# A two-layer adaLN network on one core: last stage reordered around batch 0, small weights turned earlier, rank in three operations

## The reference, cut to what matters

```python
x = x + ga * L0_attn(h);  x = x + gb * L0_ffn(h)        # layer 0, batch 2, 512 rows, 512 wide
x = x + ga1 * L1_attn(h)                                # layer 1, 128 heads of 4+64, out @ Wo
h = layernorm(x) * (1 + cb1) + sb1
# L1_ffn(h):
base_out = h @ base_W.T + base_b                        # 512 x 512
probs = softmax(h @ router_W.T + router_b)              # 15 entries
topk_p, topk_i = top_k(probs, 8)                        # ties: lower index first
w[expert_map[topk_i]] += topk_p                         # 8 experts
hr = h @ A.T                                            # 8 experts x rank 16 = 128 columns
x = x + gb1 * (base_out + (hr * w) @ B * 2)
```

## Time and profile before

| | |
|---|---|
| median of 3 runs | 2178.25 us |
| profiled execution, its own time | 2175.61 us |
| its span | 2173.8 us |
| granted TensorE clock, mean over the span | 0.994 of full speed |
| TensorE busy | 2122.4 us (98%) |
| VectorE / ScalarE / GpSimd busy | 1732.3 / 1341.9 / 1357.7 us |
| chain that ended last, share of TensorE / VectorE | 87% / 7% |

### The profile page before, as it was taken

One profiled execution on the slowest core, in us unless ns is written; L12 is line 12 of the kernel. 1 busy time (PEld: TensorE's weight loads), 2 busy tenths in 40 slices (PEclk: granted clock), 3 DMA queues, 4 the chain that ended last, 5 costly groups with the idle time before them and its releaser, 6 DMA issues.

```text
span 2173.8 us, 42824 instructions
## 1 busy us (share of the span) xinstructions
PE 2122.4 (98%) x11276; PEld 1644.1 (76%) x11276; DVE 1732.3 (80%) x3095; ACT 1341.9 (62%) x2709; POOL 1357.7 (62%) x1621
## 2 busy tenths in 40 slices
PE   7999999999999999999999999999999999999978
PEld 4788888888886757777777777777777777777756
DVE  6787788788777758888888888888888877788764
ACT  2443443433433568888888888888888865555532
POOL 4766766766753447777777777777777721365334
PEclk9999999999999999999999999999999999999999
DMA  7010010010004153222222222222222222444441
GB/s 249 26 43 30 20 48 29 19 48 29 19 20 121 37 189 108 71 73 78 74 78 65 77 78 74 76 66 79 75 77 69 75 79 76 138 130 124 114 130 40
DMA packets 138991, 165.82 MB, mean 76 GB/s; under 512 B 30261, under 2 KB 72917, under 8 KB 138916
## 3 DMA queue, kind: packets, MB, share of 16 engines
q1 hardware_dynamic: 135076, 152.31, 24.5%
q0 software_dynamic: 3840, 12.59, 2.0%
HBM read 101.52 MB, written 29.10 MB: 60 GB/s over the span
## 4 chain that ended last, share of the span: by engine, by line
PE 87%; DVE 7%; issue 2%; ACT 1%; POOL 1%; SPq 1%; DMA 1%; DVEq 0%; ACTq 0%; POOLq 0%
PE bank L2593 12%; PE bank L2578 11%; PE bank L2600 11%; PE bank L2155 7%; PE bank L2157 7%; PE bank L2156 7%; PE bank L2510 6%; PE bank L2508 5%; PE bank L2509 5%; PE bank L2623 3%; PE bank L2633 3%; PE bank L2628 2%; DVE rope_b L1631 1%; DVE rope_a L1630 1%; DVE rope_b L1632 1%
## 5 line engine op out<-in xcount | busy, mean ns | idle before, releaser
L1934 DVE TENSOR_REDUCE mcol<-bank 128x1 fp32r<-128x512 f32 x1024 | 684.1, 687 | 186.8 <-PE bank L2578 176.7
L2593 PE MATMUL bank<-q,k 128*128 128x512 f32 x1024 | 417.9, 408 | 0.0
L2578 PE MATMUL bank<-km,q 128*128 128x512 f32 x1024 | 406.0, 397 | 3.5 <-ACT q L1374 2.5
L2600 PE MATMUL bank<-q,k 128*128 128x512 f32 x1024 | 404.0, 395 | 0.0
L2578 PEld LDWEIGHTS bank<-km,q 128*128 128x128 f32 x1024 | 317.6, 310 | 53.0 <-DVE mcol L1934 3.9
L1413 ACT ACTIVATE pT<-bank 128x512 f32<-128x512 f32 x416 | 228.1, 602 | 113.7 <-PE bank L2600 111.9
L1413 ACT ACTIVATE x<-bank 128x512 f32<-128x512 f32 x416 | 227.7, 601 | 88.7 <-PE bank L2600 86.5
L2593 PEld LDWEIGHTS bank<-q,k 128*128 128x128 f32 x1024 | 192.3, 188 | 84.7 <-issue 27.9
L2600 PEld LDWEIGHTS bank<-q,k 128*128 128x128 f32 x1024 | 192.9, 188 | 31.7
L2510 PE MATMUL bank<-hT_hi,wr_lo 128*128 128x512 f32 x512 | 205.5, 401 | 0.0
L2508 PE MATMUL bank<-hT_hi,wr_hi 128*128 128x512 f32 x512 | 202.3, 395 | 0.1
(11 more groups left out here) (372 smaller groups left out, 5061.5 us busy)
## 6 DMA issues: line engine op xcount, KB each, us to landing
q<-q SPq DMA_DIRECT2D x256, 128.0 KB, 2.3
wst<-in_L_attn_Wq_rope SPq DMA_DIRECT2D x64, 256.0 KB, 3.1
o_d<-ost SPq DMA_DIRECT2D x63, 256.0 KB, 3.1
st_q<-in_L_attn_wq SPq DMA_DIRECT2D x8, 1024.0 KB, 7.6
st_wo<-in_L_attn_wo SPq DMA_DIRECT2D x8, 1024.0 KB, 5.4
q<-qc_d SPq DMA_DIRECT2D x256, 32.0 KB
km<-kc_d SPq DMA_DIRECT2D x256, 32.0 KB
k<-kc_d SPq DMA_DIRECT2D x256, 32.0 KB
```

Of the source, the lines that this page charges most:

```text
L1934: dve.tensor_reduce(mcol[:, k % 2, i % 4, i // 4:i // 4 + 1], bank[4 + i % 2][:], AX.X, ALU.max, negate=True)\
L2578: pe.matmul(bank[4 + i % 2][:], q2[:, k % 4, h, i % 4:S:4], km[:, b, h], start=True, stop=True).then_inc(max_mm, 1)
L2593: pe.matmul(bank[s % 4][:], k1[:, k % 2, t], q1[:, k % 4, h], start=True, stop=False)
L2600: pe.matmul(bank[s % 4][:], k2[:, k % 2, h, t], q2[:, k % 4, h], start=False, stop=True).then_inc(scores1, 1)
```

## The change

Four things change, all in the last 100 us.

1. Order. The last sums of batch 0 are loaded first, then x of batch 0, then the sums of batch 1, then x of batch 1. All four `first_heads` and `last_heads` of batch 0 stand ahead of those of batch 1, and the norm and the router of batch 0 ahead of the `last_heads`, respectively the norm, of batch 1. VectorE divides the last sums of batch 1 only behind the rows of norm(3, 0).
2. Small weights. `la` and `rw` have new places in SBUF, are loaded right behind `bw` and share its semaphore; they are turned ahead of the last base weights. The first three `turn_base` stand ahead of the last unit's `sum_unit`. `lb` alone is turned later, behind router(0), and its low part stands behind norm_rows(3, 1).
3. Low rank. ScalarE copies the result of `low_rank_in` to SBUF (`low_rank_copy`) in place of the spread weights (`kept_spread`); VectorE then multiplies in one operation with the factor 2. The normed columns of batch 0 lie in `hT_lo` (high and low parts), those of batch 1 in `hT_hi`.
4. Rank. One subtraction, one comparison with a margin (0 for a lower index, the smallest normal number otherwise) and the count replace two comparisons, a product, a sum and the count.

```diff
+TURN_IN, TURN_OUT, TURN_ROUTER = 4, 5, 6
+TURN_BANKS = (4, 5, 6, 7, 0, 5, 2)
+TURNS1 = (0, 1, 2, TURN_IN, TURN_ROUTER, 3, TURN_OUT)
+HIGH1 = (TURN_IN, 0, 1, 2, 3, TURN_OUT)
+LOW1 = (TURN_IN, TURN_ROUTER, 0, 1, 2, 3, TURN_OUT)
 
...
 
+            def reload_x(b):
+
+                for t in range(TB * b, TB * b + TB):
+                    sp.dma_start(x[:, t], x_d[:, t]).then_inc(x_moved[1 - b], 16)
+
             for u in range(LOOP, UNITS + 1):
                 if u == UNITS - 1:
                     load_last_sums(0)
+                if u == UNITS:
+                    sp.wait_ge(pv1, UNITS - 1)
+                    reload_x(0)
                     load_last_sums(1)
                 period(u, u % 4)
                 if u == UNITS - 5:
@@ -688,15 +717,14 @@
                     sp.wait_ge(qr_mm, UNITS)
                     sp.wait_ge(wr_split, PAIRS)
                     sp.dma_start(bw[:], a["L1_ffn_base_W"].rearrange("(k p) d -> p k d", p=P)).then_inc(wr_loaded[0], 16)
-
-            sp.wait_ge(pv1, UNITS - 1)
-            for t in range(NT):
-                sp.dma_start(x[:, t], x_d[:, t]).then_inc(x_moved[1 - t // TB], 16)
+                    sp.wait_ge(max_mm, 8 * UNITS)
+                    sp.dma_start(la[:], a["L1_ffn_A"].rearrange("e r d -> (e r) d")).then_inc(wr_loaded[0], 16)
+                    sp.dma_start(rw[0:NR], a["L1_ffn_router_W"]).then_inc(wr_loaded[0], 16)
+
+            reload_x(1)
 
 
             sp.wait_ge(o_copied, COPIES)
-            sp.dma_start(la[:], a["L1_ffn_A"].rearrange("e r d -> (e r) d")).then_inc(g_loaded, 16)
-            sp.dma_start(rw[0:NR], a["L1_ffn_router_W"]).then_inc(g_loaded, 16)
             for k in range(KT):
                 sp.dma_start(lb[:, k], a["L1_ffn_B"].rearrange("e (k p) r -> k p e r", p=P)[k]).then_inc(g_loaded, 16)
...
                 act.activation(lh_hi[:, b * S:(b + 1) * S], lh[:, b * S:(b + 1) * S], ACT.Copy).then_inc(r_hhi, 1)
 
+            weights_high1(TURN_IN)
             weights_high1(0)
             weights_high1(1)
             weights_high1(2)
             weights_high1(3)
             sums_high(EARLY)
-            sums_high(EARLY + 1)
             norm_std(3, 0)
-            weights_high1(KT)
-            weights_high1(KT + 1)
             norm(3, 0, (0,))
             norm(3, 0, (1,))
+            norm(3, 0, (2,))
+            sums_high(EARLY + 1)
+            norm(3, 0, (3,))
+            weights_high1(TURN_OUT)
+            router_parts(0)
+            low_rank_copy(0)
             norm_std(3, 1)
-            norm(3, 0, (2,))
-            norm(3, 0, (3,))
             norm(3, 1, (4,))
             norm(3, 1, (5,))
             norm(3, 1, (6,))
             norm(3, 1, (7,))
-            router_parts(0)
             router_parts(1)
+            low_rank_copy(1)
             router_exp()
             kept_turned(0)
             kept_turned(1)
-            kept_spread(0)
-            kept_spread(1)
             low_rank_high(0)
             low_rank_high(1)
...
-                dve.tensor_tensor(cmpg[:], p_m, p_n, ALU.is_gt)
-                chain(dve.tensor_tensor(cmpe[:], p_m, p_n, ALU.is_equal))
-                chain(dve.tensor_tensor(cmpe[:], cmpe[:], before[:].unsqueeze(1).broadcast_to([P, NT, NR, NR]), ALU.mult))
-                chain(dve.tensor_tensor(cmpg[:].rearrange("p t n m -> p (t n m)"), cmpg[:].rearrange("p t n m -> p (t n m)"),
-                                        cmpe[:].rearrange("p t n m -> p (t n m)"), ALU.add))
+                chain(dve.tensor_tensor(cmpe[:], p_m, p_n, ALU.subtract))
+                chain(dve.tensor_tensor(cmpg[:], cmpe[:], margin[:].unsqueeze(1).broadcast_to([P, NT, NR, NR]), ALU.is_ge))
...
             def low_rank_scaled(b):
 
-                dve.wait_ge(r_wexp, b + 1)
-                dve.wait_ge(r_hmm, b + 1)
-                dve.tensor_tensor(lh[:, b * S:(b + 1) * S], bank[1 + b][:], wexp[:, b * S:(b + 1) * S], ALU.mult).then_inc(r_hfull, 1)
+                at = slice(b * S, (b + 1) * S)
+                dve.wait_ge(r_copied, 2 * b + 2)
+                dve.wait_ge(r_wmm, b + 1)
+                dve.scalar_tensor_tensor(lh[:, at], bank[(4, 7)[b]][:], SCALING, lri[:, at], ALU.mult, ALU.mult).then_inc(r_hfull, 1)
 
             def low_rank_low(b):
 
...
             dve.memset(rwT[:], 0.0).then_inc(g_const, 1)
+            weights_low1(TURN_IN)
+            router_weights()
             weights_low1(0)
-            weights_low1(1)
-            weights_low1(2)
-            weights_low1(3)
             last_den(0)
...
+            weights_low1(2)
             gate_attention1(0)
             gate_attention1(1)
-            last_normed(1)
             add_attention1(1)
             gate_attention1(2)
-            last_sums_low(1)
+            norm_stats(3, 0, (0,))
             gate_attention1(3)
-            norm_stats(3, 0, (0,))
             add_attention1(3)
-            gate_attention1(4)
+            weights_low1(3)
             norm_stats(3, 0, (1,))
             norm_stats(3, 0, (2,))
             norm_stats(3, 0, (3,))
+            norm_rows(3, 0)
+            last_den(1)
+            last_normed(1)
+            norm_split(3, 0, (0,))
+            last_sums_low(1)
+            gate_attention1(4)
+            norm_split(3, 0, (2,))
             gate_attention1(5)
-            norm_rows(3, 0)
-            norm_stats(3, 1, (0,))
             add_attention1(5)
             gate_attention1(6)
+            norm_stats(3, 1, (0,))
+            gate_attention1(7)
+            add_attention1(7)
             norm_stats(3, 1, (1,))
-            weights_low1(KT)
-            gate_attention1(7)
-            weights_low1(KT + 1)
             norm_stats(3, 1, (2,))
-            add_attention1(7)
-            norm_split(3, 0, (0,))
             norm_stats(3, 1, (3,))
...
             behind_sums(*turn_at(LOOP))
+            def turn_base(i):
+
+                if i == 0:
+                    pe.wait_ge(wr_loaded[0], 16 * (PAIRS // 2) + 48)
+                    pe.wait_ge(q1_split, UNITS)
+                if i == KT - 1:
+                    pe.wait_ge(o_copied, COPIES)
+                for o in range(KT):
+                    e = pe.transpose(g_bank(i)[:, o * P:(o + 1) * P], bw[:, o, i * P:(i + 1) * P], ident[:])
+                e.then_inc(g_tr, 1)
+
+            def turn_low_rank(i):
+
+                if i == TURN_OUT:
+                    pe.wait_ge(g_loaded, 16 * 9)
+                    pe.wait_ge(wo1_gated, TURN_BANKS[TURN_OUT] + 1)
+                for k in range(KT):
+                    if i == TURN_IN:
+                        e = pe.transpose(g_bank(i)[:, k * P:(k + 1) * P], la[:, k * P:(k + 1) * P], ident[:])
+                    elif i == TURN_OUT:
+                        e = pe.transpose(g_bank(i)[:, k * P:(k + 1) * P], lb[:, k].rearrange("p e r -> p (e r)"), ident[:])
+                    else:
+                        e = pe.transpose(g_bank(i)[:, k], rw[0:NR, k * P:(k + 1) * P], ident[0:NR, 0:NR])
+                e.then_inc(g_tr, 1)
+
             for u in range(LOOP + 1, UNITS + 1):
+                if u == UNITS:
+                    turn_base(0)
+                    turn_base(1)
+                    turn_base(2)
                 before_sums(*turn_at(u))
                 behind_sums(*turn_at(u))
 
 
             def first_heads(t):
                 at = slice(t * P, (t + 1) * P)
-                if t >= KT:
-                    pe.wait_ge(g_lo, t - KT + 1)
+                if t in TURN_BANKS:
+                    pe.wait_ge(g_lo, LOW1.index(TURN_BANKS.index(t)) + 1)
                 for k in range(KT - 1):
                     pe.matmul(bank[t][:], oo_hi[:, k, at], wo1_hi[:, k], start=(k == 0), stop=False)
                     pe.matmul(bank[t][:], oo_hi[:, k, at], wo1_lo[:, k], start=False, stop=False)
...
+            turn_low_rank(TURN_IN)
+            turn_low_rank(TURN_ROUTER)
             turn_base(3)
             pe.wait_ge(wo1_split, KT)
             pe.wait_ge(oo_split, 6)
             first_heads(1)
-            first_heads(5)
+            first_heads(3)
+            first_heads(0)
             first_heads(2)
-            first_heads(0)
-            first_heads(4)
-            last_heads(0)
-            last_heads(1)
-            last_heads(2)
-            first_heads(3)
-            first_heads(6)
-            last_heads(3)
-            last_heads(4)
-            first_heads(7)
-            last_heads(5)
-            last_heads(6)
-            last_heads(7)
-            turn_low_rank(KT)
-            turn_low_rank(KT + 1)
-            norm(3, 0, (0,))
-            norm(3, 0, (1,))
-            norm(3, 0, (2,))
-            norm(3, 0, (3,))
-            turn_low_rank(KT + 2)
-            norm(3, 1, (4,))
-            norm(3, 1, (5,))
-            norm(3, 1, (6,))
-            norm(3, 1, (7,))
+            for t in range(TB):
+                last_heads(t)
+            for t in range(TB, NT):
+                first_heads(t)
+            norm(3, 0)
```

(15 more changed lines are left out.)

152 lines of the change are left out of this document (68 added, 84 removed).

## The result

The changed kernel takes 2185.37 us (median of 7 runs, 2183.42 to 2190.96), the kernel before in the same comparison 2177.45 us (median of 7, 2171.51 to 2180.17). The ratio is 1.0047, 95% interval [1.0031, 1.0062]: 10.2 us slower, 6.8 to 13.5. The ratio goes by the means of the seven runs, 2186.48 and 2176.34 us; the medians lie 7.9 us apart. The forecast was 2183.3 us, 5.05 slower. The direction was right, and the four idle times stand where they were forecast.

A forecast was written before the change was run, and what follows sets the result against it. Only the last stage counts, its end set by `router(1)`'s start, the matmuls behind it and new gaps. +10.4 - 8.5 + 1.8 + 0.9 + 0.3 = +4.9, said 5.0: median 2183.3 us, range 2176 to 2188.

The forecast's parts named there:

- the likeliest case: The forecast itself, with both holes followed by a slow clock: +4.4 to +6.5 us, chance 0.35.
- A: Up to the first matmul with Wo: turns wait 3.5 us for `bw`, slow clock costs 1.7; 2086.6, 4.3 us late.
- B: End of batch 0's part on TensorE: 84 matmuls take 19.7 us to 2106.3, transposes end at 2108.3.
- C: TensorE's new hole ahead of `last_heads(4)`: 5.5 us idle until VectorE's low part at 2113.8, 1.2 GHz expected behind it.
- D: Scaling batch 1's rows: ScalarE's root waits behind the copy of `low_rank_in(0)`; ready at 2128.4, before at 2121.8.
- E: Start of `router(1)`: transposes, three `base` and a slow beginning of 1.7 us put it at 2141.8, +10.4 us.
- F: Behind `router(1)`: 36 matmuls fewer, -8.5 us; exponential waits for copy and table load, new gap of 1.8 ahead of `turn_kept`.
- Tail: Last three `low_rank_out` come close together: +0.9 us for VectorE's gates waiting on GpSimd, +0.3 for two stores.
- Rival 1: TensorE's clock stays at 2.4 GHz: 7.0 us less, so -2.0, 2176.3 us; chance of no fall 0.11.
- Rival 2: Batch 0 first pays: at the turns, `bw` lands under 2078 and the clock holds; 2173.5 us, chance 0.12.
- Rival 3: Longer wait at the turns, `la` and `rw` landing at 2081.5, and longer low clock: +7 to +8, about 2186; chance 0.17.
- Rival 4: On SP's shared list batch 1's sums land about 2095, and GpSimd adds them before x's first tile: under 1 us.

The follow-up runs named there:

- a9: Changed kernel with the small loads issued in the order `rw`, `la`, `bw` in place of `bw`, `la`, `rw`: 2187.30 us, ratio 1.004 to the kernel before.
- a7: Changed kernel with TensorE kept busy in two holes (ahead of the first turn and of `last_heads(4)`) by work that changes nothing: 2183.46 us, ratio 1.0029.
- a8: a6 with batch 1's division at its old early place on VectorE and its `last_heads` ahead of `norm(3, 0)` on TensorE: 2181.03 us, ratio 1.0022.
- a6: Changed kernel with the edits of a1, a3 and a5 together: 2174.22 us, ratio 0.9987 to the kernel before.
- a5: Changed kernel with batch 1's square root ahead of the copy of `low_rank_in(0)`, and `lb`'s low part ahead of `norm_rows(3, 1)`: 2180.43 us, ratio 1.0014.
- a3: Changed kernel with the router's exponential ahead of the copy of `low_rank_in(1)` on ScalarE: 2181.99 us, ratio 1.003.
- c1: a6 with loads ordered `rw`, `bw`, `la`, a semaphore for `la` alone, and `sums_high` of batch 1 one norm column earlier: 2176.25 us, ratio 0.9991.
- a1: Changed kernel with the first three base-weight turns behind the last `sum_unit` again: 2183.28 us, ratio 1.0035.
- a2: Changed kernel with a semaphore of its own for `rw`, waited for only at the turn of `rw`: 2184.43 us, ratio 1.0044.
- c2: a6 with the rank in five operations again: 2180.05 us, ratio 1.0011 to the kernel before.
- b1: Kernel before with only the rank shortened to three operations: 2177.07 us against 2176.21, ratio 1.0006.

## Why the prediction was half right

The measured median lies in the range of 2176 to 2188 us, but outside the likeliest case's own 2182.6 to 2185, and 10.2 us is outside its +4.4 to +6.5. The sum of the forecast was +5.0 for the profiled execution. Counted from the last scores, the last stage is 9.3 us longer. The 4.3 us between are in three terms: 2.0 up to `router(1)`, 1.8 from there to the last matmul, 0.5 in the tail.

- **A, the wait at the turns: right place, wrong load, and this is the first step that failed.** Forecast was an idle time of 3.5 us, ended by `bw`; it was 5.58, ended by `rw`. Two terms were wrong and partly cancelled, which is luck. `bw` was taken at 9.1 us and took 6.3: it landed 0.7 us behind the last scores, so this term was 2.8 too high. `la` and `rw` were taken at nothing, and the wait went on for them for 4.9 us more. I had bounded their cost by 0 and 1.0 and taken 0, "as the nearest row is their own": 5.3 us from issue to landing. That row was of `rw` at another place on SyncE's list, behind 256 KB of `la`. Behind `bw` and `la` it took 10.2. In every run each of the three landed behind the one issued before it (2.8, 3.8 and 9.6 us from issue in a9, where they were issued from 2073.93 to 2074.76). The Trainium skill, "DMA: Bandwidth & Descriptors", section "Queues, rings and completion order", says that each of the 16 DMA engines takes its descriptors in ring order and that a completion lands only behind that engine's earlier writes. I had read this as an order of whole loads and put 1.0 us on it. The section does not promise so much: by it completion need not follow the order of issue where a later transfer uses fewer of these engines. The trace agrees with the order in all thirteen profiles, and the price was 2.1 us beyond the forecast. The slow clock there was taken at 1.7 and is 1.3 (a7).
- **B held.** The first matmul with Wo came at 2087.17 (forecast 2086.6) and the transposes of batch 0 at 2106.85 (2106.3): 19.7 us between them, as summed.
- **C held.** 6.00 us of idle time against 5.5, ended by the low part of the last sums, and 1.2 GHz behind it. Whether an earlier division would pay is open: in a8 it came with another order on TensorE, and the kernel was 7.6 us slower than a6.
- **D: the place held, the cause was another.** TensorE waited for the low part of `lb` until 2129.24 (forecast 2128.4). The forecast blamed the copy of `low_rank_in(0)` ahead of the root for 1.7 us (2124.2 against 2122.5) and gave the low part its own 0.6. But VectorE's variance came later than forecast, so that the copy held the root up by 0.33 us, and the low part took away the overlap of the transposes with the scaled tiles. Undone (a5), `router(1)` comes 2.6 us earlier in the profile, most of it by the low part, and 7.2 us return by the ratio, with an error of 4.
- **E, the start of `router(1)`.** 2142.33, forecast 2141.8; but behind the last scores +66.7 against +54.3, 12.4 later, where 10.4 was forecast. The difference is A's 2.1. That the absolute time fits is due to attention's 1.5 us.
- **F: the gap was right, a low clock behind it was left out.** 1.71 us of idle time ahead of `turn_kept` (forecast 1.8), with the table load right behind the copy. The rest of the 1.8 us is a fall to 1.2 GHz from 2162 to 2166: from `turn_kept` to the end of the last matmul it is 16.3 us, in a6 without a fall 14.6. I had weighed the clock at three holes and not here. That the gap caused this fall is not shown: a3, a8 and c1 have no gap there, the same fall, and the same 16.2 us; of the kernels without the gap only a6 and the one before kept the clock in their profiles. What the gap goes with is a longer slow stretch: 17.7 to 17.8 us in a1, a2, a5, a7 and a9, and in c2. "The 4.4 us taken off the rank thus don't reach the end" holds for the old order (b1) and not for the new one: with the exponential in front they are worth 5.2 us (c2 against a6). For the changed kernel itself the forecast's own sum speaks against it, since its 13.3 us against 11.3 already has the shorter rank in it; with `kept` ending the gap, a longer rank would lengthen it. That was not run.
- **ScalarE's table load.** The Trainium skill, "ScalarE: Activation LUTs", section "What ACT_TABLE_LOAD costs", would have added 1380 ns of drain. The load took 1.28 us and the exponential started 0.02 us behind it; the trace disagrees again.
- **Tail.** From the last matmul to the end 6.2 us against 4.5, +1.7 where +1.2 was forecast.
- **Rivals.** Rival 1 (no fall of the clock) fell: every one of the four holes had one. Rival 2 (batch 0 first pays) fell as stated: `bw` did land under 2078, at 2076.3, but the two small loads on its semaphore took its place, so its own condition was the wrong one. The same landing was one of the two signs by which the forecast called itself wrong; it came, and for station A rightly so. Rival 3 is what happened, for its first half: `rw` at 2081.2 (it named 2081.5) and a longer low clock, at a place it did not name. The measured 2185.37 us is nearer to its 2186 than to the forecast's 2183.3. Rival 4: the sums of batch 1 were added at 2094.3, no sign of a cost.

The three undone steps turn the loss into a small gain together (a6, 13.1 us by the ratio, with an error of 4); what each is worth rests on the profiles, 4.3, 2.6 and 1.8 us, one execution each. The order "batch 0 first" as such, with the small weights early, then stands at 1.0011 [1.0, 1.0022] (c2, with the old rank): no gain, and hardly a loss. With the short rank it is 0.9987. What stays open is why `rw`, 30 KB, lands 3.9 us behind `la` in one execution (a5) and 0.2 in another (a2), with the same loads around it; why the clock fell behind 0.33 us of idle time in a3, a8, b1 and c1 and not in a6; what each of the two swaps of a5 is worth by itself; and whether an early division pays.

## What to carry to other kernels

When a step is put ahead on one engine, look at what now stands behind it in that engine's list, and at what a wait covers. The low part of `lb` behind four scaled tiles kept TensorE from its first transpose, up to 2.6 us, and a copy that waits for 12 matmuls, ahead of an exponential, cost 1.9 us; moving them back cost nothing. A copy that finds the next operation waiting for something else as well costs only the difference (0.33 us here, not the 1.7 forecast). The landing time of a load belongs to its place in the queue, not to the load; do not let the first work wait on a semaphore that counts a small load issued last. Count a low clock behind each new gap, but only up to the next point where another engine comes later anyway, and look for it in several profiles: here it came and went by 1.6 us in kernels with no gap at all.

## What the runs showed of the hardware

- A load of 30 KB took 2.8 us when it was issued first (a9, c1) and 7.2 to 10.3 us behind 1.25 MB (7.2 in a8, 10.3 in a5 and a6). Whichever of the three stood last took 7.2 to 10.3 us (`bw` 9.6 in a9, `la` 7.3 in c1).
- The length of an idle time alone did not tell the granted clock behind it. The turns ran at 1.00 behind 2.93 us (a3) and at 0.50 behind 3.01 (a6). It fell to 0.5 behind the 1.7 us ahead of `turn_kept` in all six kernels that have them, and in four without them, behind 0.33 us (a3, a8, b1, c1); behind two of 0.7 us with short work between them (a6) it stayed at 1.00. Work that changes nothing, put into the holes, kept it at 1.00 in them (a7).
- A function table load took 1.28 us and the next operation started 0.02 us after it.
